# Final part of a two-layer kernel: sums moved to TensorE, scaling to ScalarE, powers after the gathers

## The reference

```python
xn = _layernorm(x)                      # kept as xn1_all
s = chebyshev_attention(xn)             # s1_all holds s / 2
logits = xn @ router_w.T + router_b     # 8 experts, the best 2 of each token
topk_w = softmax(topk_vals)
out = 0
for e in range(8):
    cw = sum(where(topk_idx == e, topk_w, 0))
    y = gelu(xn @ w1[e].T + b1[e]) @ w2[e].T + b2[e]
    out = out + y * cw
out = layernorm(out + xn) * ln_w + ln_b
x = x + s * silu(out)
```

## Time and profile before

| | us |
|---|---|
| median of 3 runs | 802.78 (802.03 to 805.84) |
| profiled execution, whole | 805.15 |
| its span | 803.3 |
| VectorE busy | 649.7 (81%) |
| TensorE busy, weight loads | 575.8 (72%), 387.0 |
| GpSimd busy | 433.4 (54%) |
| ScalarE busy | 419.9 (52%) |

### The profile page before, as it was taken

One profiled execution on the slowest core, in us unless ns is written; L12 is line 12 of the kernel. 1 busy time (PEld: TensorE's weight loads), 2 busy tenths in 40 slices (PEclk: granted clock), 3 DMA queues, 4 the chain that ended last, 5 costly groups with the idle time before them and its releaser, 6 DMA issues.

```text
span 803.3 us, 22093 instructions
## 1 busy us (share of the span) xinstructions
PE 575.8 (72%) x6987; PEld 387.0 (48%) x7049; DVE 649.7 (81%) x1675; ACT 419.9 (52%) x1019; POOL 433.4 (54%) x697
## 2 busy tenths in 40 slices
PE   1889888888887888886134799899999986452231
PEld 0466666666665655664012456555666553231120
DVE  4678888888788778875279899999999999966687
ACT  1465555555454455452023888888988883211011
POOL 3235555555455778773774445444544453778810
PEclk9999999999799999996557999999999997655555
DMA  9999999900000000000122133333333321212201
GB/s 213 364 284 288 288 285 287 257 0 0 1 0 7 16 21 17 20 17 4 40 102 69 32 115 115 123 107 112 113 107 105 107 67 47 53 52 55 69 27 40
DMA packets 126475, 80.84 MB, mean 101 GB/s; under 512 B 10936, under 2 KB 117312, under 8 KB 126400
## 3 DMA queue, kind: packets, MB, share of 16 engines
q1 hardware_dynamic: 121264, 70.89, 29.4%
q0 software_dynamic: 5136, 9.02, 4.1%
HBM read 18.85 MB, written 49.55 MB: 85 GB/s over the span
## 4 chain that ended last, share of the span: by engine, by line
DVE 42%; PE 20%; issue 16%; POOL 13%; ACT 5%; DVEq 1%; DMA 1%; SPq 1%; POOLq 0%; ACTq 0%
POOL experts_sb L561 8%; DVE kv L1356 4%; DVE yts L1383 4%; DVE mneg L1128 3%; DVE kv L1366 3%; PE q_ps L940 3%; DVE yn L1387 3%; DVE kv L1357 2%; POOL xbuf L490 2%; PE y_ps L873 2%; DVE pr L1381 2%; DVE rot L1170 2%; ACT pexp L608 2%; PE m_ps L823 1%; PE m_ps L809 1%
## 5 line engine op out<-in xcount | busy, mean ns | idle before, releaser
L608 ACT ACTIVATE pexp<-e_ps 128x512 f32<-128x512 f32 x128 | 76.4, 597 | 70.8 <-PE e_ps L856 67.6
L1128 DVE TENSOR_REDUCE mneg<-m_ps 128x4 bf16<-128x512 f32 x128 | 84.9, 684 | 18.7 <-PE m_ps L823 18.4
L561 POOL DMA_INDIRECT experts_sb<-ybuf,slots x64 | 64.1, 1002 | 31.2 <-issue 18.8
L1033 PE MATMUL m_ps<-xs,wb 128*128 128x512 f16 x276 | 74.4, 379 | 3.0 <-ACT xs L726 3.0
L490 POOL DMA_INDIRECT xbuf<-x,slots x64 | 64.4, 1006 | 16.6 <-issue 15.4
L996 PE MATMUL y_ps<-kv,tri_sb 128*128 128x432 f32 x64 | 36.3, 653 | 38.3 <-DVE pr L1382 25.2
L873 PE MATMUL y_ps<-pexp,vd 128*32 128x128 f32 x512 | 57.8, 295 | 2.4 <-ACT pexp L608 0.6
L1087 PE MATMUL e_ps<-b_sb,cwt 8*128 8x128 f32 x64 | 16.6, 436 | 52.3 <-ACT cwt L766 52.3
L837 PE MATMUL e_ps<-early 128*128 128x256 bf16 x256 | 51.6, 283 | 0.8 <-DVE early L1213 0.6
L498 POOL COPY xn_all<-early 128x128 f32<-128x128 f32 (+1 forms) x32 | 12.8, 399 | 71.4 <-DVE early L1138 71.4
L555 POOL TENSOR_TENSOR pexp<-rot,pexp 128x512 f16<-128x512 f32 x24 | 28.9, 1204 | 40.3 <-ACT pexp L718 40.1
(11 more groups left out here) (220 smaller groups left out, 2056.0 us busy)
## 6 DMA issues: line engine op xcount, KB each, us to landing
xbuf<-zero_sb SPq DMA_DIRECT2D x71, 256.0 KB, 4.0
ybuf<-zero_sb SPq DMA_DIRECT2D x71, 256.0 KB, 3.6
wb<-experts_sb SPq DMA_DIRECT2D x46, 256.0 KB, 2.3
xs<-xbuf SPq DMA_DIRECT2D x23, 256.0 KB, 2.7
ybuf<-vd SPq DMA_DIRECT2D x23, 256.0 KB, 2.2
experts_sb<-in_experts_w SPq DMA_DIRECT2D x8, 512.0 KB, 6.8
x_all<-in_x SPq DMA_DIRECT2D x8, 256.0 KB, 5.6
xbuf<-x,slots POOLq DMA_INDIRECT x64, 2.3
```

The lines of the kernel that those rows point to most:

```text
L561: nc.gpsimd.indirect_dma_start(yg[:, 2 * (B * n + b) + k, :], None, ybuf, bass.IndirectOffsetOnAxis(ap=slots[:, k, B * n + b:B * n + b + 1 ...
L608: nc.scalar.activation(pexp[:, j, :, :], e_ps[j % 2][:, :, :], ACT.Exp, scale=float(D) ** -0.5).then_inc(exp_ready.sem, 1)
L1033: last = nc.tensor.matmul(u_ps[f % 2], wb1[:, i % 2, f, a, :], xg16[:, i % 2, b, :], start=k == 0, stop=k == len(PARTS) - 1)
L1128: nc.vector.tensor_reduce(mneg[:, n.batch, j // 2, (j % 2) * NG:(j % 2) * NG + NG], m_ps[j % 2][:, :, :], AX.X, ALU.max, negate=True).then ...
```

## The change

The combination is no longer made by VectorE in SBUF. TensorE's residual(n) multiplies xn1_all with an identity into one of three PSUM banks (the two of d_ps and t_ps) and adds the four bias products there; ScalarE's weigh_rows(n) multiplies the eight gathered tiles by their weights in place; TensorE's sum_rows(n) adds them through the identity. VectorE's spread(n) takes the statistics from PSUM, GpSimd raises to the power (groups 0 to 2 in one instruction, later groups after the next-but-one gather), VectorE's centre(n) makes -mean * rstd, ScalarE's normalise(n) writes y2, and VectorE's gate(n) runs three groups behind. The turning of weights, their copy and the residual of groups 0, 1 and 2 stand at the end of Chebyshev tiles 29, 30 and 31. Small arrays move into the space of logits, and y2, e2 get two buffers each.

```diff
-GATE = 5
+GATE = 4
+SHARED = 3
...
+        a_ps = [d_ps[0], d_ps[1], t_ps[:, :, :]]
...
@@ gpsimd
+            def deviation(lo, hi):
+                tiles = slice(B * lo, B * hi)
+                pool.wait_ge(s_spread, B * hi)
+                nc.gpsimd.tensor_tensor(rstd2[:, 0, tiles], mv2[:, tiles, 1], eps2_sb[:, tiles], ALU.add).then_inc(s_rstd2, 1)
+                powers[0] += 1
+                pool.wait_ge(s_rstd2, 2 * powers[0] - 1)
+                nc.gpsimd.tensor_tensor(rstd2[:, 1, tiles], rstd2[:, 0, tiles], half_sb[:, 0:1].to_broadcast([P, B * (hi - lo)]), ALU.pow).then_inc(s_rstd2, 1)
             for n in range(5):
                 gather(n)
-            for n in range(TAUS):
-                deviation(n)
-                if n + 5 < TAUS:
-                    gather(n + 5)
+            deviation(0, SHARED)
+            for n in range(SHARED, TAUS):
+                if n + 2 < TAUS:
+                    gather(n + 2)
+                deviation(n, n + 1)
@@ scalar
+            def weigh_rows(n):
+                act.wait_ge(s_gathered[n], 16 * 2 * B)
+                for k in range(2):
+                    for b in range(B):
+                        rows = yg[:, n, k, b * C:b * C + C]
+                        nc.scalar.activation(rows, rows, ACT.Copy, scale=rs[:, 7 - k, B * n + b:B * n + b + 1]).then_inc(s_weighted, 1)
+            def normalise(n):
+                act.wait_ge(s_shift2, n + 1)
+                after(act, s_result, n - 1)
+                for b in range(B):
+                    t = B * n + b
+                    nc.scalar.activation(y2[n % 2][:, b, :], a_ps[n % 3][:, b, :], ACT.Identity, scale=rstd2[:, 1, t:t + 1], bias=shift2[:, t:t + 1]).then_inc(s_normed, 1)
+            def tangent(n):
+                act.wait_ge(s_gate, GATE * n + 2)
+                nc.scalar.activation(e2[n % 2], y2[n % 2], ACT.Tanh, scale=0.5).then_inc(s_tanh, 1)
             for c in range(NT):
...
                 if c + 2 < NT:
                     polynomials(c + 2)
+                if c >= NT - SHARED:
+                    cw_copy(c - NT + SHARED)
             oc_copy(NT - 1)
             s1_copy(NT - 1)
...
+            for n in range(SHARED):
+                weigh_rows(n)
+            for n in range(SHARED, TAUS + 2):
+                if n < TAUS:
+                    cw_copy(n)
+                normalise(n - SHARED)
+                if n < TAUS:
+                    weigh_rows(n)
+                if n > SHARED:
+                    tangent(n - SHARED - 1)
+            normalise(TAUS - 1)
+            tangent(TAUS - 2)
+            tangent(TAUS - 1)
@@ tensor
+            def turn_weights(n):
+                after(pe, s_cw_copied, n - 1)
+                for b in range(B):
+                    last = nc.tensor.transpose(m_ps[n % 2][0:E, b, :], cw[:, B * n + b, :], eye_sb[:, :])
+                last.then_inc(s_cw_transposed, 1)
+            def residual(n):
+                pe.wait_ge(s_cw_copied, n + 1)
+                after(pe, s_normed, B * (n - 2))
+                a = a_ps[n % 3]
+                nc.tensor.matmul(a, eye_sb[:, :], xn1_all[:, B * n:B * n + B, :], start=True, stop=False, skip_group_check=True)
+                for b in range(B):
+                    last = nc.tensor.matmul(a[:, b, :], cwt[:, n % 2, b, :], b2_sb[:, :], start=False, stop=False, skip_group_check=True)
+                last.then_inc(s_bias_summed, 1)
+            def sum_rows(n):
+                pe.wait_ge(s_weighted, 2 * B * (n + 1))
+                for k in range(2):
+                    last = nc.tensor.matmul(a_ps[n % 3], eye_sb[:, :], yg[:, n, k, :], start=False, stop=k == 1, skip_group_check=True)
+                last.then_inc(s_mixed, 1)
             for c in range(NT):
...
                 down(i, 3)
+                if c >= NT - SHARED:
...
+                    turn_weights(n)
+                    residual(n)
             transpose_out(NT - 1)
             project_out(NT - 1)
-            for n in range(TAUS):
-                bias_terms(n)
+            for n in range(SHARED):
+                sum_rows(n)
+            for n in range(SHARED, TAUS):
+                turn_weights(n)
+                residual(n)
+                sum_rows(n)
@@ vector
-            def combine(n):
...
+            def spread(n):
+                a = a_ps[n % 3]
+                dve.wait_ge(s_mixed, n + 1)
...
+                    nc.vector.bn_stats(stats2[:, n % 2, b, :], a[:, b, :]).then_inc(s_stats2, 1)
...
+                    nc.vector.bn_aggr(mv2[:, B * n + b, :], stats2[:, n % 2, b, :]).then_inc(s_spread, 1)
+            def centre(n):
+                tiles = slice(B * n, B * n + B)
+                dve.wait_ge(s_rstd2, 2 * max(n - SHARED + 2, 1))
+                nc.vector.scalar_tensor_tensor(shift2[:, tiles], mv2[:, tiles, 0], -1.0, rstd2[:, 1, tiles], ALU.mult, ALU.mult).then_inc(s_shift2, 1)
             def gate(n):
...
-                dve.wait_ge(s_rstd2, 2 * n + 2)
-                for b in range(B):
-                    last = nc.vector.tensor_scalar(y2[:, b, :], a[:, b, :], m[:, b, 0:1], rstd2[:, n % 2, 1, b:b + 1], ALU.subtract, ALU.mult)
-                done(last)
+                dve.wait_ge(s_normed, B * (n + 1))
...
             dve.wait_ge(s_s1_copied, NT)
-            for n in range(TAUS):
-                combine(n)
-                if n:
-                    gate(n - 1)
-            gate(TAUS - 1)
+            for n in range(SHARED):
+                spread(n)
+            centre(0)
+            for n in range(SHARED, TAUS):
+                centre(n - 2)
+                spread(n)
+                gate(n - SHARED)
+            for n in range(TAUS - SHARED, TAUS):
+                if n + 1 < TAUS:
+                    centre(n + 1)
+                gate(n)
```

More of the change, by code:

```diff
@@ L269, in program @@
         w16 = experts_sb[:, :, :].bitcast(F16).rearrange("p k (s c) -> p k s c", s=2)
-        res1, acc1 = (gel[i].rearrange("p (b c) -> p b c", b=B) for i in range(2))
-        res, acc = [res0, res1], [acc0, acc1]
-        yg = experts_sb
+        res1, e3 = (gel[i].rearrange("p (b c) -> p b c", b=B) for i in range(2))
+        res, y2, e2 = [res0, res1], [y2, y3], [e2, e3]
+        yg = experts_sb[:, :, :].rearrange("p (n k b) c -> p n k (b c)", k=2, b=B)
         u_ps = [m_ps[i][:, :, :].rearrange("p a b -> p (a b)") for i in range(2)]
@@ L560, in gather @@
                     for k in range(2):
-                        nc.gpsimd.indirect_dma_start(yg[:, 2 * (B * n + b) + k, :], None, ybuf,
+                        nc.gpsimd.indirect_dma_start(yg[:, n, k, b * C:b * C + C], None, ybuf,
                                                      bass.IndirectOffsetOnAxis(ap=slots[:, k, B * n + b:B * n + b + 1], axis=0)).then_inc(s_gathered[n], 16)
[L564 to L569, removed]
+            powers = [0]
+            def deviation(lo, hi):
[5 more added lines that the diff above has]
+                nc.gpsimd.tensor_tensor(rstd2[:, 1, tiles], rstd2[:, 0, tiles], half_sb[:, 0:1].to_broadcast([P, B * (hi - lo)]), ALU.pow).then_inc(s_rstd2, 1)
             for n in range(8):
@@ L734, in y_copy, with cw_copy @@
                 nc.scalar.copy(ysb[:, i % 2, :, :], d_ps[i % 2]).then_inc(s_y_copied, 1)
+            def cw_copy(n):
+                act.wait_ge(s_cw_transposed, n + 1)
+                after(act, s_bias_summed, n - 1)
+                nc.scalar.copy(cwt[:, n % 2, :, :], m_ps[n % 2][0:E, :, :]).then_inc(s_cw_copied, 1)
+            def weigh_rows(n):
[13 more added lines that the diff above has]
+                nc.scalar.activation(e2[n % 2], y2[n % 2], ACT.Tanh, scale=0.5).then_inc(s_tanh, 1)
             v_copy(0)
@@ L1074, in _ @@
                 down(i, 3)
+                if c >= NT - SHARED:
+                    n = c - NT + SHARED
+                    if n == 0:
+                        pe.wait_ge(s_gelu, 2 * FB * PASSES)
+                        pe.wait_ge(s_y_copied, PASSES)
+                    turn_weights(n)
+                    residual(n)
             transpose_out(NT - 1)
             project_out(NT - 1)
-            def bias_terms(n):
-                after(pe, s_cw_copied, n - 1)
-                for b in range(B):
[L1082 to L1091, removed]
-            for n in range(TAUS):
-                bias_terms(n)
+            for n in range(SHARED):
[4 more added lines that the diff above has]
+                sum_rows(n)
         @block.vector
@@ L1403, in _ @@
                     weights_of_two()
-            def combine(n):
[L1407 to L1418, removed]
+            def spread(n):
+                a = a_ps[n % 3]
+                tiles = slice(B * n, B * n + B)
+                dve.wait_ge(s_mixed, n + 1)
+                after(dve, s_spread, B * (n - 1))
                 for b in range(B):
-                    dve.wait_ge(s_mixed, 2 * B * n + B + b + 1)
-                    nc.vector.bn_stats(stats2[:, b, :], a[:, b, :]).then_inc(s_stats2, 1)
```

(7 more changed lines are left out.)

40 lines of the change are left out of this document (16 added, 24 removed).

## The result

The changed kernel takes 798.74 us (median of 5 runs, 796.29 to 799.92). The kernel before was run twice more beside it and has now a median of 805.84 (802.03 to 806.94). The ratio estimated from all executions is 0.9904, with a 95% interval of 0.9879 to 0.9929 (the two medians alone give 0.991): 1% faster, where 0.6% was forecast (797.8 against 802.78). The profiled execution is the fastest of its five, 796.29 with a span of 794.5.

What follows compares the result with a forecast made beforehand. VectorE was taken to bound the kernel before, TensorE's queue at a mixed clock the changed one. R 734.5 plus 47.8 less 2.8 gives S 779.5, plus 18.8 a span of 798.3, as a median 797.8; range 786 to 808.

Steps and rivals of the forecast that it cites:

- The bound: Final part: VectorE, 9.7 us a group, would need 4.9; TensorE becomes slower at low clock, 10.1 us a group.
- The prices: Costs assumed per operation in the final part, such as 1.75 us for a 512-column TensorE matmul at 1.2 GHz.
- Tiles 29 to 31: Last Chebyshev tiles: moved turns and residuals delay the sums; last s1_copy ends at 720.8, or 719.4 with one clock rise.
- R: Start of residual(3) on TensorE, after the first three sums of rows and the first power: expected at 734.5.
- S: End of sum_rows(7), the last sum of rows, set by TensorE's queue: expected at 779.5.
- From S to the end: VectorE's last statistics, four gates and three centres, then the store: 18.8 us.
- The clock: TensorE, final part: rises after some sum_rows, falls in the pause; one rise every two groups, worth about 1.4 us; chance 0.47.
- All at 1.2 GHz: Rival: TensorE's clock stays low through tiles 29 to 31 and the final part; end 805.2, chance 0.22.
- Clock up, gathers the bound: Rival: high clock in most of the final part, GpSimd's gathers set the time; end 786, chance 0.23.
- The powers don't lag: Rival: GpSimd waits for statistics before each gather group; 1 or 2 us at most, about 800, within the 0.47 mixed case.

Runs made afterwards that it cites:

- the yardstick: The changed kernel itself, unaltered, run once more on the chip of the follow-up kernels: 797.0 us, ratio 0.9888 to the kernel before.
- the first experiment: Against the changed kernel, turning, copy and residual of groups 0 to 2 put back behind the last Chebyshev projection: 808.52 us, ratio 1.0037 to the kernel before.

## Why the prediction was right

*The bound.* That VectorE would be relieved and TensorE's queue, with its waits for ScalarE, take its place was right: VectorE waits 2 to 3 us for the sums of each group from 4 on, and the pair without gathers shows that GpSimd doesn't bind.

*The prices.* The 512-column matmul at 1.2 GHz, put at 1.75, takes 1.79 in the sums (3.57 for two) and 2.01 as own rows (694.75 to 696.76), beyond the upper bound of 1.86. Eight weighings take 2.4 (2.2), four normalisings 1.5 (1.15), TensorE's wait 2.14 (1.87), the twelve-column power 2.31 (2.15). All were a little too low, and no table load came on top of those of before.

*Tiles 29 to 31.* residual(0) was expected at 695.8 and sums(30) at 699.6; they came at 694.75 and 698.76, and ScalarE's polynomials before them ended 1.1 sooner in this execution than in that of before. sums(31), at 1.2 GHz expected at 709.35, came at 706.53, with the clock up in residual(1). The last s1_copy ended at 715.44, expected 719.4: 1.1 is the earlier start, the rest the clock: two rises, together worth 4.3, where I had counted one of 1.4. In the yardstick there is one, from the turn of group 2 on. That the delay would be worth paying was not asked in the prediction; the first experiment answers it, by 11.5 us.

*R and S.* R was 730.4, expected 734.5: 4.0 from s1_copy, and the three sums took 6.8 for 7.8, against dearer weighing, power and normalising. The first gather of group 5 so went out at 728.71, ahead of the 731 to 737 given (730.48 in the yardstick). S - R was 45.9, expected 45.0: the clock rose once in every group instead of every second, which the dearer matmuls and the longer wait took back. From S to the end 18.2, expected 18.8. Sum: 794.5 for 798.3, in the fastest of five executions; the median one of the five has a span of 796.9, 1.4 off.

*Luck in the number.* The median of 797.8 (measured 798.74) holds two things that cancel by chance. Clock rises more frequent than forecast took back what dearer matmuls, weighing and waits cost. And the 2.37 us by which I set the median below the profiled execution came from only three executions of the kernel before: with five its median is 805.84, above its profiled 805.15. Without that step the forecast is 800.2, and as a ratio, 798.3 to 803.3 of span, still 0.994.

*The clock.* That the clock goes up at the end of some sum_rows and comes down in the pause behind holds for the rise and, between the groups, not for the fall. The clock stayed up through the pauses of 2.14 us and fell in the own rows or bias behind them, 0.6 to 1.7 us into the group; that is why those own rows are fast, which the price of the forecast (turn and part of the next residual) had allowed for. How often it rises was off as well: four times at the four hand-overs between groups 3 and 7 of this execution and three times in the yardstick, where I had reckoned with two. The rule of the Trainium skill quoted there (TensorE: Matmul & The Clock Gate, "HAM oscillation — how this bites in real kernels") has each burst start slow. The trace agrees behind the longer pause of 5.34 us (own rows 2.04 at 730.40) and not behind those of 2.14, where the bursts start fast and slow down later. The kernel with filled pauses shows what the low clock costs here: about 5 us, after which another queue binds.

*The rivals.* "All at 1.2 GHz" (805.2) did not occur here; the kernel with residuals behind the last tile, 0.50 for 17 us, shows that such stretches exist. "Clock up, gathers the bound" was right in its mechanism, seen in the kernel with filled pauses and in those with the turn ahead, but its 786 rested on a fast clock in tiles 29 to 31 as well: with the final part alone fast the time is 792.0. "The powers don't lag" stayed small for the later groups, as reckoned (GpSimd waits 0.72 for the statistics of group 3); its wait for the first statistics is 2.21 in this execution and 7.01 in the yardstick.

## What to carry to other kernels

When work moves to an engine that was idle, price it at the clock of that stretch and in its queue: the three large matmuls of a group cost 5.6 us at 1.2 GHz, but the hand-overs around them 2.1 more, and an order that has the next group's small steps done first got those back. Work laid into another stage's end can pay even if it delays that stage: here it did, because the work behind is bound by the same queue. After each repair ask which queue is next: here TensorE, then the gathers, which set the time up to the last sum; what stands behind it can still be shortened, as the gate before the statistics shows.

## What the runs showed that I had not expected

In the kernel with residuals behind the last tile TensorE was busy 15.11 of 17.10 us at 0.50 throughout; own rows of 2.0 us stood between pieces with 8 rows or columns and breaks of 0.67. In the sums directly behind, 7.2 us without a break, the clock rose (0.73 on average). No run here separates the kind of work from the breaks.

Small GpSimd operations take longer beside VectorE's wide ones: the addition of four columns took 0.21 alone and 0.69 when it began with VectorE's L1501. It then ended at 764.70, 0.05 behind L1501; three others, of 0.55 and 0.56, ended 0.05 to 0.06 behind an L1495. That GpSimd waits for the VectorE instruction is argued from these times; no run isolates it.

```profile
752.40 0.21 POOL L575 TENSOR_TENSOR logits<-logits 128x4 f32<-128x4 f32 x1
...
764.01 0.69 POOL L575 TENSOR_TENSOR logits<-logits 128x4 f32<-128x4 f32 x1
```

```profile
763.96 0.69 DVE L1501 TENSOR_TENSOR xs<-xs,x_all 128x512 f32<-128x512 f32 x1
```
